# Running sums of the decay as three bf16 parts, a second buffer for the transposed y, and a new order of the state part

## What is computed

```python
dt = softplus(dt_raw + dt_bias); a = dt * A
cum = jnp.cumsum(a, axis=2)                      # running sums in the chunk
diff = cumT[..., :, None] - cumT[..., None, :]
decay = jnp.where(mask, jnp.exp(jnp.where(mask, diff, 0.0)), 0.0)
scores = jnp.einsum('bclhg,bcshg->bchls', Cc, Bc) * decay * dtT[:, :, :, None, :]
Y_intra = jnp.einsum('bchls,bcshp->bclhp', scores, Xc)
S = jnp.einsum('bcshg,bcshp->bchgp', Bc * w[..., None], Xc)   # w = exp(cum_last - cum) * dt
H = exp(cum_last) * H + S                        # carried from chunk to chunk
Y_inter = jnp.einsum('bclhg,bchgp->bclhp', Cc * jnp.exp(cum)[..., None], Hprev)
y = rmsnorm((Y_intra + Y_inter + D_skip[:, None] * Xc) * silu(z), gnorm_w)
out = y @ out_proj_w.T
```

## Time and profile before

| | |
|---|---|
| median of three runs | 2977.33 us (2972.32 to 2981.53) |
| the profiled execution | 2979.97 us, its span 2978.3 us |
| TensorE busy | 2761.3 us, 93% of the span |
| VectorE busy | 2529.3 us, 85% |
| GpSimd busy | 1917.9 us, 64% |
| ScalarE busy | 1724.8 us, 58% |
| mean granted TensorE clock | 0.982 of full speed |
| data moved by DMA | 34.24 MB, 3.5% of the DMA engines' time |

### The profile page before, as it was taken

The page is one execution under the profiler, slowest core; times in us unless marked ns, Lnnn a source line. Parts: engine busy times, 40 slices in busy tenths (PEclk is TensorE's granted clock), DMA queues, the critical chain, the costliest instruction groups (busy, mean ns, idle before and its releaser), DMA issues.

```text
span 2978.3 us, 50716 instructions
## 1 busy us (share of the span) xinstructions
PE 2761.3 (93%) x15168; PEld 2276.2 (76%) x15168; DVE 2529.3 (85%) x6406; ACT 1724.8 (58%) x3560; POOL 1917.9 (64%) x2328
## 2 busy tenths in 40 slices
PE   5899999999999999999999999999999999999985
PEld 4777887787877787887777777778777878777863
DVE  4598888988888988888988888988889888888985
ACT  4465665665565655665665666555556555665642
POOL 2276666676667676666676666666666766675755
PEclk9999999999999999999999999999999999999998
DMA  3000000000000000000000000000000000000000
GB/s 127 8 8 12 5 11 7 11 11 11 7 7 7 11 11 11 4 10 7 11 11 11 4 11 7 11 11 11 4 7 11 11 11 11 4 7 11 8 4 7
DMA packets 28183, 34.24 MB, mean 11 GB/s; under 512 B 2672, under 2 KB 27248, under 8 KB 27440
## 3 DMA queue, kind: packets, MB, share of 16 engines
q1 hardware_dynamic: 28144, 33.77, 3.5%
HBM read 25.37 MB, written 8.39 MB: 11 GB/s over the span
## 4 chain that ended last, share of the span: by engine, by line
PE 39%; DVE 32%; issue 12%; POOL 10%; ACT 6%; DVEq 1%; DMA 0%; ACTq 0%; SPq 0%; POOLq 0%
PE bank L1336 13%; DVE acc L1003 11%; POOL Em L531 8%; PE bank L1551 4%; PE bank L1516 4%; PE bank L1492 4%; PE bank L1468 3%; DVE Em L1163 3%; PE bank L1355 3%; PE bank L1543 2%; DVE Em L1172 2%; DVE acc L993 2%; DVE v L1069 2%; PE products L1501 1%; ACT acc L690 1%
## 5 line engine op out<-in xcount | busy, mean ns | idle before, releaser
L1003 DVE SCALAR_TENSOR_TENSOR acc<-bank,cw,acc 128x253 f32<-128x253 f32 (+2 forms) x1920 | 773.7, 470 | 0.0
L1336 PE MATMUL bank<-hT,w_in 128*128 128x256 f32 x2560 | 608.3, 383 | 13.0 <-DVE acc L1003 12.3
L1336 PEld LDWEIGHTS bank<-hT,w_in 128*128 128x128 f32 x2560 | 484.7, 192 | 119.7 <-issue 44.5
L531 POOL TENSOR_TENSOR Em<-ee 128x1024 f32<-128x1024 f32 x256 | 513.4, 2026 | 46.8 <-issue 46.5
L1163 DVE SCALAR_TENSOR_TENSOR Em<-Em,p 128x1024 f32<-128x1024 f32 x256 | 435.0, 1699 | 0.0
L546 POOL TENSOR_TENSOR W<-W,Em 128x1024 f32<-128x1024 f32 x128 | 336.1, 2626 | 8.5 <-ACT Em L818 0.3
L818 ACT ACTIVATE Em<-Em,rden 128x1024 f32<-128x1024 f32 x256 | 291.4, 1142 | 73.5 <-DVE Em L1172 73.5
L690 ACT ACTIVATE acc<-bank,cb,cw 128x256 f32<-128x256 f32 x640 | 325.6, 562 | 0.0
L1172 DVE TENSOR_TENSOR Em<-Em,products 128x1024 f32<-128x1024 f32 x256 | 311.1, 1215 | 4.5
L671 ACT ACTIVATE xbcT<-acc 128x512 f32<-128x512 f32 x320 | 200.3, 626 | 140.4 <-DVE acc L1003 140.3
L1501 PE MATMUL products<-w_de,h2T 128*128 128x512 f32 x512 | 235.0, 602 | 23.8 <-DVE Em L1172 23.8
(11 more groups left out here) (177 smaller groups left out, 5594.1 us busy)
## 6 DMA issues: line engine op xcount, KB each, us to landing
x_in<-x_dram SPq DMA_DIRECT2D x32, 256.0 KB, 2.7
x_res<-x_dram SPq DMA_DIRECT2D x32, 256.0 KB, 2.7
out_dram<-f SPq DMA_DIRECT2D x32, 256.0 KB, 2.2
w_in<-in_wT_dram SPq DMA_DIRECT2D x1, 3080.0 KB, 12.9
w_up<-upT_dram SPq DMA_DIRECT2D x1, 1024.0 KB, 15.5
w_de<-down_eT_dram SPq DMA_DIRECT2D x1, 1024.0 KB, 17.5
w_down<-downT_dram SPq DMA_DIRECT2D x1, 1024.0 KB, 19.5
w_ue<-up_e_dram SPq DMA_DIRECT2D x1, 1024.0 KB, 21.6
```

Source lines behind the costliest of these rows:

```text
L531: nc.gpsimd.tensor_tensor(Em[:, k], bc(ee[:, k, 0:XD], 2, KEYS), bc(ee[:, k, XD:XD + KEYS], 1, XD), ALU.mult).then_inc(E_done.sem, 1)
L1003: ins = V.scalar_tensor_tensor(acc[:, r, a, ahead:], ps[:, a * TOK:(a + 1) * TOK - ahead], cw[:, t, k:k + 1], acc[:, r, a, ahead:], ALU.mu ...
L1336: last = mm(ring[j % 2][:, a * TOK:(a + 1) * TOK], w_in[:, k, at:at + P], hT[:, k, :], start=k == 0, stop=k == DK - 1)
```

## The change

Five things change.

1. The rows. `da` is written four times side by side into 128 columns (each copy of 16 columns with 16 zero columns behind it). One more matmul on TensorE, `da` as weights and the triangle as moving data, gives the running sums transposed: row 32 b + k of `cumT` holds those of chunk and head k. ScalarE copies them to SBUF, and GpSimd splits them in `mixer_parts` into three bf16 parts whose sum is exact (rows 32 on: first part; 64 on: second; 96 on: third). `mixer_rows` then multiplies `pick`, a bf16 column that chooses the three parts of one head, by `cum_parts`, in bf16.
2. `yT` has one copy for each chunk.
3. The order of TensorE: X and rows of chunk 1 stand behind the scores of chunk 0; S of chunk 0 behind Yn of chunk 0; the transposes of y stand one before and one behind Yn and S of chunk 1, and both projections at the end.
4. The order of VectorE, ScalarE and GpSimd follows: on VectorE pair 9's convolution stands ahead of the second `ffn_best`, the first gate ahead of `ffn_stats`, and `ffn_store` behind the third `ffn_times`; on ScalarE `ffn_out` stands behind the second decay, and the `yT` copies stand between the experts; on GpSimd `mixer_scale(g, 1)` stands ahead of `tail_root`.
5. The program is built with a DMA scratch of 8192.

```diff
-        da = sb("da", [P, CH, HEADS])
+        da = sb("da", [P, 4, 2 * CH * HEADS])
-        yT = sb("yT", [P, INNER])
+        yT = sb("yT", [P, CH, INNER])
@@ GpSimd: mixer_dt
-                nc.gpsimd.tensor_tensor(da[:], dts[:], bc(neg_a[:], 1, CH), ALU.mult).then_inc(da_done.sem, 1)
+                nc.gpsimd.tensor_tensor(dta[:], dts[:], bc(neg_a[:], 1, CH), ALU.mult).then_inc(own_pool, own.one())
+                pool.wait_ge(own_pool, own.n)
+                nc.gpsimd.tensor_copy(da[:, :, 0:CH * HEADS], bc(dta[:].rearrange("p c h -> p (c h)"), 1, 4))\
+                    .then_inc(da_done.sem, 1)
@@ GpSimd: new
+            def mixer_parts(g):
...
+                nc.gpsimd.tensor_copy(cum_parts[:], cumT[:]).then_inc(own_pool, own.one())
+                nc.gpsimd.tensor_scalar(cum_rest[:], cum_parts[:], minus_a[:, 0:1], None, ALU.mult)\
+                nc.gpsimd.tensor_tensor(cum_rest[:], cum_rest[:], cumT[:], ALU.add).then_inc(own_pool, own.one())
+                nc.gpsimd.tensor_copy(cum_parts[:], cum_rest[:]).then_inc(own_pool, own.one())
+                nc.gpsimd.tensor_scalar(cumT[:], cum_parts[:], minus_b[:, 0:1], None, ALU.mult)\
+                nc.gpsimd.tensor_tensor(cum_parts[:], cum_rest[:], cumT[:], ALU.add).then_inc(parts_done.sem, 1)
@@ GpSimd: do_group
                 if a:
                     mixer_cum(g)
+                    mixer_parts(g)
...
+                if a:
+                    mixer_scale(g, 1)
                 if c:
                     tail_root(f, statsf, mvf, vf, rsf, rootf)
                 if a:
-                    mixer_scale(g, 1)
                     mixer_decay(g, 1)
@@ ScalarE: mixer_cum, mixer_yT
+                nc.scalar.activation(cumT[:], yb[:, P:2 * P], ACT.Copy).then_inc(cum_sb.sem, 1)
-                if c or later(g):
-                    act.wait_ge(out_ps.sem, out_ps.at(g, c - 1))
-                nc.scalar.activation(yT[:], pairb[c][:], ACT.Copy).then_inc(yT_sb.sem, 1)
+                if later(g):
+                    act.wait_ge(out_ps.sem, out_ps.at(g - 1, c))
+                nc.scalar.activation(yT[:, c], pairb[c][:], ACT.Copy).then_inc(yT_sb.sem, 1)
@@ ScalarE: do_group
                 if a:
                     mixer_B(g, 0)
-                if c:
-                    ffn_out(f)
                 if n is not None:
                     mixer_hT(n)
                 if a:
                     mixer_move(g, 1)
                     mixer_decay(g, 1)
+                if c:
+                    ffn_out(f)
+                if a:
                     mixer_B(g, 1)
                     mixer_square(g, 0)
                 if b:
                     tail_keep(e)
-                    ffn_experts(e, 0, 0, 1)
+                    ffn_experts(e, 0, 0)
                 if a:
                     mixer_yT(g, 0)
+                if b:
+                    ffn_experts(e, 0, 1)
+                if a:
+                    mixer_yT(g, 1)
                     mixer_square(g, 1)
-                    mixer_yT(g, 1)
-                if b:
-                    ffn_experts(e, 0, 2)
-                if b:
-                    ffn_experts(e, 0, 3)
+                if b:
+                    ffn_experts(e, 0, 2, 3)
@@ VectorE: do_group
-                conv(7, 8)
+                conv(7, 8, 9)
                 if b:
                     ffn_best(e, 1)
-                conv(9)
...
-                if c:
-                    ffn_stats(f)
                 if a:
                     mixer_state(g, 0)
                     mixer_scores(g, 0)
                 if b:
                     ffn_last(e, 0)
                     ffn_mask(e, 0, 0)
                 if a:
+                    mixer_gate(g, 0)
+                if c:
+                    ffn_stats(f)
+                if a:
                     mixer_step(g, 0)
+                if b:
+                    ffn_times(e, 0, 0)
+                if a:
+                    mixer_scores(g, 1)
+                if b:
+                    ffn_mask(e, 0, 1)
+                if a:
+                    mixer_state(g, 1)
+                if b:
+                    ffn_times(e, 0, 1)
+                    ffn_mask(e, 0, 2)
+                if a:
+                    mixer_gate(g, 1)
+                    mixer_step(g, 1)
+                if b:
+                    ffn_times(e, 0, 2)
                 if c:
                     ffn_store(f)
-                if a:
-                    mixer_gate(g, 0)
-                if b:
-                    ffn_times(e, 0, 0)
-                    ffn_mask(e, 0, 1)
-                if a:
-                    mixer_scores(g, 1)
-                if b:
-                    ffn_times(e, 0, 1)
-                if a:
-                    mixer_state(g, 1)
-                if b:
-                    ffn_mask(e, 0, 2)
-                if a:
-                    mixer_gate(g, 1)
-                if b:
-                    ffn_times(e, 0, 2)
-                if a:
-                    mixer_step(g, 1)
                 if b:
                     ffn_mask(e, 0, 3)
                     ffn_times(e, 0, 3)
@@ TensorE: mixer_cum, mixer_rows
+                mm(yb[:, P:2 * P], da[:].rearrange("p a b -> p (a b)"), tri[:], start=True, stop=True)\
+                if c == 0:
+                    pe.wait_ge(parts_done.sem, parts_done.at(g))
-                        last = mm(pairb[q][:, i * P:(i + 1) * P], da[:, c, h:h + 1].to_broadcast([P, P]), tri[:],
+                        k = c * HEADS + h
+                        last = mm(pairb[q][:, i * P:(i + 1) * P], pick[:, k:k + 1].to_broadcast([P, P]), cum_parts[:],
@@ TensorE: do_group
                     mixer_scores(g, 0)
-                    mixer_S(g, 0)
-                    mixer_Yn(g, 0, e, n)
                     mixer_X(g, 1)
                     mixer_rows(g, 1, f)
+                    mixer_Yn(g, 0, e, n)
+                    mixer_S(g, 0)
                     mixer_B(g, 1)
                     mixer_scores(g, 1)
                     mixer_Yi(g, 1)
+                    mixer_yT(g, 0)
                     mixer_Yn(g, 1, e, n)
-                    mixer_yT(g, 0)
                     mixer_S(g, 1)
+                    mixer_yT(g, 1)
                     mixer_out(g, 0)
-                    mixer_yT(g, 1)
                     mixer_out(g, 1)
@@ build
-    nc = bacc.Bacc("TRN2", target_bir_lowering=False, num_devices=1)
+    nc = bacc.Bacc("TRN2", target_bir_lowering=False, num_devices=1, dynamic_dma_scratch_size=8192)
```

More of the change, by code:

```diff
@@ L150, in sandwich @@
         dts = sb("dts", [P, CH, HEADS])
-        da = sb("da", [P, CH, HEADS])
+        da = sb("da", [P, 4, 2 * CH * HEADS])
+        cumT = sb("cumT", [P, P])
+        cum_rest = sb("cum_rest", [P, P])
+        cum_parts = sb("cum_parts", [P, P], BF16)
+        minus_a = sb("minus_a", [P, 1])
+        minus_b = sb("minus_b", [P, 1])
+        pick = sb("pick", [P, CH * HEADS], BF16)
         cum = sb("cum", [P, 3, CH, HEADS])
@@ L332, in _ @@
             nc.gpsimd.memset(H[:], 0.0).then_inc(own_pool, own.one())
+            nc.gpsimd.memset(da[:], 0.0).then_inc(own_pool, own.one())
+            nc.gpsimd.memset(pick[:], 0.0).then_inc(own_pool, own.one())
+            nc.gpsimd.memset(minus_a[:], -1.0).then_inc(own_pool, own.one())
+            nc.gpsimd.memset(minus_b[:], -1.0).then_inc(own_pool, own.one())
             nc.gpsimd.memset(minus1[:], -1.0).then_inc(own_pool, own.one())
@@ L347, in _ @@
                 .then_inc(own_pool, own.one())
+            for first, minus in ((64, minus_a), (96, minus_b)):
+                nc.gpsimd.affine_select(out=minus[:], in_=minus[:], compare_op=ALU.is_ge, fill=0.0,
+                                       base=-first, pattern=[[0, 1]], channel_multiplier=1)\
+                    .then_inc(own_pool, own.one())
+            for block in range(3):
+                pool.wait_ge(own_pool, own.n)
+                nc.gpsimd.affine_select(out=pick[:], in_=pick[:], compare_op=ALU.not_equal, fill=1.0,
+                                       base=-32 * (block + 1), pattern=[[-1, CH * HEADS]], channel_multiplier=1)\
+                    .then_inc(own_pool, own.one())
             pool.wait_ge(own_pool, own.n)
@@ L1232, in do_group @@
                 if a:
+                    mixer_gate(g, 0)
+                if c:
+                    ffn_stats(f)
+                if a:
                     mixer_step(g, 0)
-                if c:
-                    ffn_store(f)
-                if a:
-                    mixer_gate(g, 0)
                 if b:
                     ffn_times(e, 0, 0)
-                    ffn_mask(e, 0, 1)
                 if a:
@@ L1250, in do_group @@
                     mixer_gate(g, 1)
+                    mixer_step(g, 1)
                 if b:
                     ffn_times(e, 0, 2)
-                if a:
-                    mixer_step(g, 1)
+                if c:
+                    ffn_store(f)
                 if b:
@@ L1346, in mixer_cum @@
                 n = CH * HEADS
```

(7 more changed lines are left out.)

15 lines of the change are left out of this document (13 added, 2 removed).

## The result

The changed kernel takes 3047.84 us (median of four runs, 3046.97 to 3048.85); the kernel before, run beside it on the same chip, 2976.64 us. The ratio is 1.0239, with a 95% interval of 1.0221 to 1.0257: slower by 71 us, where 101 were forecast. It is on the forecast side and inside the range.

What follows compares the result with a forecast made beforehand. TensorE (93% busy) and VectorE (85%) were near their limit, but nobody was full in a group's last stretch, a chain of waits. 2980 + 30 x (1.6 + 2.6) - 25 = 3081, less 2.6: 3078 us; range 2975 to 3150.

Steps and rivals of the forecast that it cites:

- The first half: Last stretch of a group, to the first gate: rows at 949.1, `ffn_out` 950.0, gate 962.7 instead of 970.77.
- The store's end: VectorE's queue from first gate through `ffn_store`: ends at 978.8, between 976.6 without GpSimd collisions and 981.2.
- The added wait: ScalarE's copy to `x1_late` waits for `ffn_store`; next first convolution at 989.7 against 988.14, 1.6 us more a group.
- Rival E: ScalarE's wait isn't on the path: 4.4 us less a group, about 2845 us; chance 0.05.
- Rivals C and D: C: store at 977.2, no change, 0.07. D: store by 976.6, clock stays, 30 x -0.5, 2962 us, 0.10.
- The clock: TensorE idles 7 us before the first projection in every group, its clock falls: 2.6 us more a group.
- Rival B: The wait is there but the clock doesn't fall more often: 30 x 1.6, about 3028 us; chance 0.16.
- The 25 us that the sum took off: Nine clock falls already in the kernel before, 9 x 2.85 us, subtracted as contained in the new term.
- The first two parts: A group from first convolution to 940.30, TensorE full: the new `cumT` matmul adds 0.22 us a group in full.
- twice that price would be hidden too: Six GpSimd operations of `mixer_parts`, 1.7 to 2.4 us plus gaps, hidden in 11.5 us of GpSimd idle time.
- The gain that the change is sure of: 16 row matmuls on TensorE go from fp32 to bf16: 0.67 us for each of four banks, 2.7 a group.
- The two copies of `yT` buy nothing here: ScalarE's `yT` copies before the output projections: no gain, the second copy is ready before the first projection ends.

Runs made afterwards that it cites:

- the late-copy kernel: The changed kernel with ScalarE's copy to `x1_late` (`tail_keep`) moved behind three of the four `ffn_experts`: 2834.14 us, ratio 0.9472 to the kernel before.
- the best version: The late-copy kernel with the first output projection ahead of the second transpose of y on TensorE: 2819.97 us, ratio 0.9459.

## Why the prediction was right, and where it was wrong

Times of the kernel after are set against the forecast by taking 19.97 us off: the ninth of the ten convolutions starts at 960.54 after and at 940.35 before, and the forecast's times have 0.22 us for `cumT` in them, so 940.57.

**The first half: right.** The rows start at 969.08, shifted 949.1 (forecast 949.1), `ffn_out` on TensorE at 969.96, shifted 950.0 (950.0), and the first gate at 982.91, shifted 962.9 (962.7). TensorE, GpSimd and VectorE in the timeline of the kernel after:

```profile
969.08 0.38 PE L1420 MATMUL bank<-mask_b,ident_b 128*128 128x512 bf16 x1
...
969.29 0.39 PE L1424 MATMUL bank<-cum_parts,pick 128*128 128x128 bf16 x4
...
969.52 0.38 PE L1420 MATMUL bank<-mask_b,ident_b 128*128 128x512 bf16 x1
...
969.96 3.67 PE L1600 MATMUL bank<-w_ue,WT 128*128 128x256 f32 x16
...
977.14 1.90 POOL L573 TENSOR_TENSOR Em<-ee 128x1024 f32<-128x1024 f32 x1
...
980.00 7.05 POOL L573 TENSOR_TENSOR Em<-ee 128x1024 f32<-128x1024 f32 x3
...
980.07 2.92 DVE L1210 SCALAR_TENSOR_TENSOR Em<-Em,p 128x1024 f32<-128x1024 f32 x1
982.91 0.67 DVE L1087 TENSOR_TENSOR yv<-yv,bank 128x512 f32<-128x512 f32 x1
983.62 1.68 DVE L1090 TENSOR_TENSOR yv<-yv,zs 128x512 f32<-128x512 f32 x1
...
989.06 1.27 DVE L1210 SCALAR_TENSOR_TENSOR Em<-Em,p 128x1024 f32<-128x1024 f32 x1
...
991.98 1.33 DVE L1210 SCALAR_TENSOR_TENSOR Em<-Em,p 128x1024 f32<-128x1024 f32 x1
```

Four row matmuls go in 0.23 us (969.29 to the mask at 969.52), as forecast.

**The store's end: right in time, wrong in which operations collide.** The forecast was 978.8; the store's last operation ends at 998.72, shifted 978.75. But the forecast had a mask and the store collide with GpSimd between the first gate and the store's end. The rows show neither: the two masks there take 1.27 and 1.33 us, and the store's two tensor_scalars 0.72 where they took 2.25. (The mask of 2.92 us stands ahead of the gate, outside that sum.) In their place the second product of each gate takes 1.68 us. The group of this line says that it holds in the whole run (busy us, mean ns):

```profile
L1090 DVE TENSOR_TENSOR yv<-yv,zs 128x512 f32<-128x512 f32 x64 | 105.5, 1649 | 2.2
```

The forecast had put 2.2 us of collisions on its 976.6, for a mask and the store; the two gates cost 1.0 each, 2.0. The sum came out right since the errors cancelled, and that was luck. The trace shows both engines slower where they work side by side. On VectorE the mask that starts at 980.07 took 2.92 us and the gate's product at 983.62 took 1.68; a mask with none of GpSimd's `Em` products beside it took 1.27 (989.06), and the gate's product took 0.69 at 94.38, in the first group, with GpSimd idle. GpSimd's three products from 980.00 on took 7.05 us, where three times the 1.90 of the one at 977.14, which had only VectorE's 0.69 us products from a PSUM bank beside it, would be 5.70. Which of the two engines holds up the other, no run tested.

**The added wait: right.** The timeline of the kernel after, from the second transpose of y to the next group's first convolution:

```profile
995.67 0.66 PE L1507 MATMUL bank<-ident,yv 128*128 128x128 f32 x4 [1.57 <-DVE yv L1090]
...
997.27 0.72 DVE L1233 TENSOR_SCALAR f<-f,mvf,rsf 128x256 f32<-128x256 f32 x2
998.03 0.69 DVE L1237 TENSOR_TENSOR f<-f,x_late 128x512 f32<-128x512 f32 x1
...
998.82 0.63 ACT L820 ACTIVATE x_late<-x 128x512 f32<-128x512 f32 x1 [12.31 <-DVE f L1237]
...
1002.78 5.76 PE L1517 MATMUL bank<-w_out,yT 128*128 128x256 f32 x16 [6.45 <-ACT yT L804]
1008.38 3.62 PE L1381 MATMUL bank<-hT,w_in 128*128 128x256 f32 x16
...
1011.69 0.35 DVE L1040 SCALAR_TENSOR_TENSOR acc<-bank,cw,halo_sum 128x3 f32<-128x3 f32 x2 [1.00 <-ACT acc L734]
```

ScalarE idles 12.31 us (some 12 forecast), TensorE 6.45 (7 forecast), the projection starts at shifted 982.81 (982.8). Rival E, by which the copy was not on the path, is out: taking it off the path is worth 7%, and the 2834.14 us that it gives are near the 2845 that E forecast for that case. Rivals C and D, a store by 977.2 or 976.6, are out by the rows above.

**The clock: right in kind, 0.5 too high in size.** The forecast's 2.6 us was its author's estimate: between 2.05, half of the 4.12 us of work in the one low stretch of the earlier trace rows, and 3.4, half of all its 6.82 us. With the bounds of the wait, -0.5 and +4.0, these two made the 1.55 and the 7.4 of its range. No run shows 2.6. The projections' two halves need 5.60 us to the start of pair 0 (1002.78 to 1008.38); at full clock, in the kernel with stand-in matmuls, 3.53 (994.29 to 997.82): 2.1 us. The clock is low for 10.24 us, longer than the 6.82 of the earlier trace rows, but with 4.17 us of work in it, hardly more than the 4.12 there. The forecast raised 2.05 because all that follows the gap is on the path; it overlooked that most of a low stretch lies over the gap itself. That the fall would come in every group was the author's assumption; the kernel before showed one behind such a gap, of 5.30 us, in the last groups. Rival B, no additional falls, is out: each of the 30 groups has one, and with the gap filled 3047.84 became 2995.86. This mis-sized term is 30 x 0.5, some 15 us of the 30 that the forecast was too high. The 25 us that the sum took off were nine falls of 2.85 us, 91.84 less 88.99; no run shows nine, the kernel before had eight in its steady groups.

The forecast laid the fall to the gap of 7 us. The clock fell at 996.72, though, 0.4 us after TensorE's last matmul ahead of that gap (the transpose at 995.67), and the late-copy kernel, which has only the wait of 1.58 us ahead of this transpose, falls at the same place for 3.4 us. So what the copy's wait adds is the length of the low stretch, 10.24 us, so that it still covers the projections, which now come later.

**The first two parts: the cost was right, a gain was left out.** The step "it costs 0.22 a group in full" gave +0.22; the first two parts together, to the ninth convolution, measured 41.02 us against 41.22, so -0.2. The matmul for `cumT` itself costs 0.30 us (957.12 to the next matmul at 957.42). What took more back is a layer norm product on VectorE at the start of a group. It comes in two lengths, in the kernel before too (two groups before, then one after):

```profile
990.74 2.26 DVE L1069 TENSOR_SCALAR v<-v,mv,rs 128x256 f32<-128x256 f32 x2
...
1083.03 1.83 DVE L1069 TENSOR_SCALAR v<-v,mv,rs 128x256 f32<-128x256 f32 x2
```

```profile
1014.29 1.83 DVE L1116 TENSOR_SCALAR v<-v,mv,rs 128x256 f32<-128x256 f32 x2
```

In the kernel before, the groups that follow a fall of the clock have the short one and first parts of 40.8 us, the others the long one and 41.2. The kernel after has the short one and 41.0 in its steady groups; the best version has the long one, 2.33 us, and 41.5. Like against like, the change costs 0.2 to 0.3 us, as forecast, and the shorter product gives 0.4 to 0.5 back. With stand-in matmuls in the gap the first parts are 41.0 also in groups that follow no fall; why the product is the short one there no run tested. 30 x 0.4, the distance from +0.22 to -0.2, is 12 us, and with the clock's 15 nearly the whole error of 30.

**`mixer_parts`: hidden, and dearer than its bound.** The six operations take 2.7 us against 1.7 to 2.4: a tensor_scalar from bf16 to fp32 took 0.61 us, and a product 0.46, above the 0.40 that the earlier trace rows gave as the dearest of 128x128. They end near 961.8, seven us before the rows. The forecast's "twice that price would be hidden too" covered it.

**"The gain that the change is sure of": wrong as a rule.** The 2.7 us a group were there where TensorE was the bound (groups of 85 against 87.5). In the old order the same edit lost 6.6, because the next thing late was VectorE's `sL`. The step read only TensorE's own records and left out what the forecast asked of each other step: what is late next, and what the gap does to the clock.

**"The two copies of `yT` buy nothing here": wrong.** The sum had credited them without saying so: it counted 1.81 us from the first projection to the next operation, without the 0.78 us that TensorE waits between the two projections in the earlier trace rows. With one copy in the changed kernel this wait is back, in a stretch at low clock, and costs 58 us. The number of the forecast was right, its sentence was not.

## What to carry to other kernels

When a step is moved later, list who waits for it on other engines and what is queued behind each of them: here one copy, waiting for a store that no longer came early, turned a 5.3% gain into a 2.4% loss. Time saved on an engine that is then next to wait isn't neutral on TensorE: the bf16 rows in the old order took 2.7 us of its work away, its wait grew from 1.3 to 4.7 us, the clock was low for 13.7 us, and the group took 6.6 us more, so price a saving together with the wait that follows it. To tell waiting from clock, fill the gap with stand-in matmuls and time again (52 and 127 us came back here); the cure was real work in the gap (14 us more won), or no wait (210 us).

## What the runs showed of the hardware

- A low-clock stretch at a gap lasted 3.4, 6.8, 10.2, 13.7 or 17.1 us in the steady groups of these kernels, and its length didn't follow the work in it: 10.24 us with 4.17 of work (the kernel after), 13.65 with 11.04 (bf16 rows in the old order).
- Small gaps could be enough: behind 1.58 us the clock stood at 0.51 for 3.41 us in six groups of eight (the late-copy kernel); with work in that gap and a wait of 0.78 us behind the second transpose, it stayed at 1.00.
- With one recurring gap lengthened from 1.3 to 4.7 us a group took 6.6 us more, more than the gap itself; with stand-in matmuls in the gap most groups took 1.2 us more.
- Bf16 matmuls whose result is unused gave back most of the clock: 52 us of 3047.84 and 127 of 3156.80. With them in the changed kernel, 15 of the 30 groups still had 3.4 us of low clock.
- VectorE's product of two SBUF operands, 128x512 fp32, took 0.69 us alone and 1.68 beside GpSimd's products of 128x1024; the gate's sum ahead of it, with one input in PSUM, stayed at 0.67 beside them.
